# Two places of count keys in a graph-network kernel: one counter for both, or one each

## The chip, the cores and the metric

The kernel runs on one core of a Trainium2 chip. What counts is the time of one execution on the device, in microseconds (us). Before the change the median of three runs is 1840.04 us (1839.89 to 1840.95).

## The reference, cut to what matters

There are 6250 nodes with 256 features and 106,250 edges, sorted by destination. `h` is the ReLU of the layer-normalized `x`. Two layers follow, and their result is added to `x`:

```python
def layer(z, l):
    logits = z @ envW[l] + envb[l]                     # 256 -> 4 experts
    weights = softmax(logits)
    agg = segment_sum(z[src], dst) / max(count(dst), 1)
    combined = concatenate([agg, z])                   # 512
    outputs = einsum('nd,kdo->nko', combined, W[l]) + z[:, None, :]
    return relu(einsum('nk,nko->no', weights, outputs))
```

The expensive parts are the mean over a node's edges (`agg`) and the product of the 512 combined features with four experts' weights.

## The kernel before, in words

Nodes are cut into 49 blocks of 128. For each block TensorE (PE) sums the neighbours' rows in one of two ways.

- **Sparse blocks** (33): the source rows of the block's edges come in units of 2 x 128 edges, fetched by indirect DMAs that GpSimd (POOL) issues into a ring of 12 units (L713, two DMAs a unit). VectorE (DVE) makes one-hot matrices of the destinations (`compare`, L865), and PE multiplies one-hot by rows (L1295, L1300, four matmuls a unit). The one-hots stand in ten places; the pair of places 7 and 8, with place 9, is filled by `compare_next(..., 2)`.
- **Dense blocks** (16): a matrix of edge counts (128 nodes of the block by all nodes) is multiplied by all node features, which lie in SBUF (`group_sum`, L1333, L1335). ScalarE (ACT) turns the counts from bytes into floats in two stage buffers (`fill_stage`, L1075).

The counts themselves are made once, in layer 0, by products of two bf16 one-hot matrices: `win_lo` (position within the block) and `win_key` (window and source). DVE makes them in `window_keys` (L916, L919). PE multiplies them window by window, two windows to a pair (`window_pair`, L1346), and ACT moves each pair from PSUM to SBUF as bytes (`move_pair`, L1087, L1090, L1092). A dense block has 13 pairs, in group 0 (7 pairs) and group 1 (6 pairs). The SBUF tiles `win_lo` and `win_key` hold one group: a **small place** (pairs 0 and 1, four windows) and a **large place** (pairs 2 and up: ten windows in group 0, eight in group 1). `window_keys(dn, g, i)` fills place `i` for group `g` of dense block `dn`; PE waits for the small place before pair 0 and for the large one before pair 2 (`s_key[0]`, `s_key[1]`). That a place may be overwritten is told by one semaphore, `s_keyfree`: ACT adds 2 when PE has summed the last pair of a group, and each fill takes 1.

Each layer has a prologue and then 16 rounds of a loop of three slots. A slot of PE's queue holds a block's eight weight products (`product(0)` to `product(7)`, L1366, two matmuls each) with the sums of the next block between them:

- `first_slot` (k = 0 on the other engines): products 2 to 7, nine or more units of the ring, and in layer 0 the six pairs of group 1: `pair(0)` stands between `product(4)` and unit 7, `pair(1)` after unit 8, `pair(2)` after `product(5)` and a tenth unit if there is one, then the transposition of the next block's features (`turn_z`, L1269), which waits for DVE's `z_in`.
- `dense_slot` (k = 1): a dense block's 49 products with counts and eight units.
- `rest_slot` (k = 2): in layer 0 the seven pairs of group 0, among the eight products, for the next round's dense block.

The order on every engine is written out by hand and static; engines wait only on semaphores. Around the change DVE's order in slot k = 0 is: read two numbers of dense blocks from SBUF (`dense_no`, L671), `take_logits` (L941, L943), `compare_next` (L865), `take_weights` (the softmax weights, L947, L948), small place of group 1, wait for ACT's scaled `z` and `keep_z` (L927, makes `z_in`), large place of group 1, `combine_half(0)` (L953). Both places of group 0 are filled in slot k = 1. In slot k = 2 there is no fill; `split` (L974, L976) stands ahead of `keep_z`. ACT's order in slot k = 2 is `move_pair(0, 0)`, `exps`, `move_pair(0, 1)`, and so on.

These are the lines of the fill that wait and signal:

```python
a, b = (0, 2) if i == 0 else (2, PAIRS_IN[g])
take(dve, s_keyfree)
```

Of the kernel before, what the change touches and what calls it, by code (L numbers as in the profile page):

```python
# [23 lines left out]
PER_ROUND = 2  # L24
# [14 lines left out]
def gnn_kernel(nc, x, src, dst, W, envW, envb, out):  # L39
# [63 lines left out]
    with ctx:  # L103
# [88 lines left out]
        s_ohr = sem("more_onehots_ready")  # L192
        s_ohf = sem("other_onehots_free")
        s_key = [sem(f"keys{i}_ready") for i in range(2)]
        s_keyfree = sem("keys_free")
        s_win = [sem(f"window_pair{p}_summed") for p in range(2)]
        s_wfree = [sem(f"window_pair{p}_free") for p in range(2)]
        s_evac = sem("window_pair_moved")
# [442 lines left out]
        with main_ctx:  # L641
# [57 lines left out]
            with nc.Block() as block:  # L699
# [71 lines left out]
                def _(dve):  # L771
# [81 lines left out]
                    dve.sem_inc(s_mixfree[0], 1)  # L853
                    dve.sem_inc(s_mixfree[1], 1)
                    dve.sem_inc(s_lgfree, 1)
                    dve.sem_inc(s_keyfree, 2)

                    others_from = dve.alloc_register("others_from")
                    others_to = dve.alloc_register("others_to")
# [49 lines left out]
                    def window_keys(dn, g, i):  # L909

                        a, b = (0, 2) if i == 0 else (2, PAIRS_IN[g])
                        take(dve, s_keyfree)
                        w = nc.s_assert_within(dve.snap(dn * WPB + 2 * (PAIR_FROM[g] + a)), 0, WINS - 2 * (b - a),
                                               skip_runtime_bounds_check_because="windows of one block")
                        n = 2 * (b - a)
                        nc.vector.tensor_tensor(  # L916
                            win_lo[:, 2 * a:2 * b, :], lo16[:].unsqueeze(1).to_broadcast([P, n, P]),
                            lo_w[:, bass.ds(w, n)].unsqueeze(2).to_broadcast([P, n, P]), ALU.is_equal)
                        nc.vector.tensor_tensor(  # L919
                            win_key[:, 2 * a:2 * b, :], key16[:].unsqueeze(1).to_broadcast([P, n, KEYS]),  # L920
                            key_w[:, bass.ds(w, n)].unsqueeze(2).to_broadcast([P, n, KEYS]),
                            ALU.is_equal).then_inc(s_key[i], 1)
# [56 lines left out]
                    for l in range(L):  # L979
# [13 lines left out]
                        take_mean(l, sparse_block(dve, zero, 0), 0)  # L993
                        compare_first(sparse_block(dve, zero, 1), wide=True)
                        compare_more()
                        with dve.Fori(0, rounds) as r:
                            dn = dense_no(dve, r)
                            dn1 = dense_no(dve, r + 1)
                            for k in range(ORDER):
                                following = sparse_block(dve, r, k + 1)  # L1000
                                take_logits(l)
                                if k == 0:
                                    compare_next(following, 2)
                                elif k == DENSE_AT:
                                    compare_next(following, 0)
                                take_weights()
                                if k == DENSE_AT:
                                    compare_next(following, 1)
                                    compare_next(following, 2)
                                if first and k == 0:  # L1010
                                    window_keys(dn, 1, 0)
                                elif k == 0:
                                    compare_rest()
                                if k == DENSE_AT + 1:
                                    compare_rest()
                                if first and k:
                                    split()
                                if not first and k <= DENSE_AT:
                                    for g in range(0 if k == 0 else FIRST_GROUPS, FIRST_GROUPS if k == 0 else XG):
                                        dve.wait_ge(s_zload[g], 16)  # L1020
                                take(dve, s_zs)
                                keep_z(block_of(dve, r, dn, k + 1))
                                if first and k == 0:
                                    window_keys(dn, 1, 1)
                                    compare_rest()
                                if first and k == DENSE_AT:
                                    window_keys(dn1, 0, 0)
                                    window_keys(dn1, 0, 1)
                                combine_half(0)
                                take_mean(l, block_of(dve, r, dn, k + 1), bank_of(k))  # L1030
                                if first and k == DENSE_AT:
                                    dve.sem_inc(s_zused, 1)
                                if k < PER_ROUND and k != DENSE_AT:
                                    compare_first(sparse_block(dve, r, k + 2 if k < DENSE_AT else k + 1))
                                elif k == PER_ROUND:
                                    more = dve.snap(r + 1)
                                    with dve.If(more < rounds):
                                        compare_first(sparse_block(dve, more, 1), wide=True)
                                combine_half(1)
                                if k == PER_ROUND:  # L1040
                                    with dve.If(more < rounds):
                                        compare_more()
                                if not first:
                                    result()
                            if first:
                                split()
# [12 lines left out]
                def _(act):  # L1059
# [18 lines left out]
                    def move_pair(g, j):  # L1078

                        p = j % 2  # L1080
                        take(act, s_win[p])
                        if j == PAIRS_IN[g] - 1:
                            act.sem_inc(s_keyfree, 2)
                        at = 2 * WIN * (PAIR_FROM[g] + j)
                        two = win_ps[p][:, 0:2 * KEYS].rearrange("p (v c n) -> p c v n", v=2, n=WIN)
                        if at + 2 * WIN <= P:
                            nc.scalar.activation(counts_sb[:, :, at:at + 2 * WIN].rearrange(  # L1087
                                "p c (v n) -> p c v n", n=WIN), two, ACT.Copy).then_inc(s_evac, 1)
                        else:
                            nc.scalar.activation(counts_sb[:, :, at:at + WIN], two[:, :, 0, :],  # L1090
                                                 ACT.Copy).then_inc(s_evac, 1)
                            nc.scalar.activation(counts_sb[:, :, at + WIN:P], two[:, :, 1, 0:P - at - WIN],  # L1092
                                                 ACT.Copy).then_inc(s_evac, 1)
                            take(act, s_evac)
                        take(act, s_evac)
                        act.sem_inc(s_wfree[p], 1)
# [461 lines left out]
```

## Time and profile before

| | |
|---|---|
| median of three runs | 1840.04 us |
| profiled execution, from its first to its last instruction (span) | 1839.2 us |
| runs' median beside that span | 0.84 us more, 0.05% |
| PE busy / POOL busy / DVE busy / ACT busy | 87% / 66% / 49% / 31% of the span |
| mean granted clock of PE | 0.969 of full speed |
| layer 0, from the first round's dense sums on | about 54.6 us a round |
| layer 1 | about 47.9 us a round |

Shares of busy time are averages over the whole execution. PE is the busiest engine. Its clock has two levels here, 2.4 GHz (1.00 in the profile) and 1.2 GHz (0.50). A bracket at the end of a row gives how long the engine stood idle before it and what ended that: "PEq L101" or "DVEq L101" is a wait on a semaphore in the engine's own queue. An engine that is idle costs nothing unless the others wait for it.

### The profile page before, as it was taken

What the parts mean: (1) busy time and instruction counts of PE and PEld (TensorE: products, weight loads), DVE (VectorE), ACT (ScalarE), POOL (GpSimd) and SP (SyncE); (2) the same over time, 40 slices, a digit from 0 to 9 for tenths busy, and PEclk for the clock granted to TensorE, in tenths of its full rate; (3) what the DMA queues carried; (4) which work ended last, traced back from release to release, by engine and by line L of the source; (5) the groups of instructions that cost most, each with busy time, mean ns of one, the idle gap of its engine ahead of it and who ended that gap; (6) DMA issues with size and microseconds to landing.
All of it is one profiled execution on the core that took longest, in us unless ns stands there. A gap on an engine that the chain in (4) does not pass through costs nothing. (4 is left out here: it accounts for less than half of the span.)

```text
span 1839.2 us, 36146 instructions
## 1 busy us (share of the span) xinstructions
PE 1598.5 (87%) x8502; PEld 1124.8 (61%) x8503; DVE 895.0 (49%) x2024; ACT 572.7 (31%) x1254; POOL 1214.2 (66%) x1187
## 2 busy tenths in 40 slices
PE   1059999999999999999998389999999999999998
PEld 1036665666666666666665266666666666667665
DVE  6665565655565565555564224334443333443333
ACT  4414333334434333433333022222222222222222
POOL 1377776766776676676663677666666666666764
PEclk9989999999999999999999599999999999999999
DMA  7877766666666666666656987677777777777775
GB/s 218 284 216 227 215 206 186 189 180 195 206 191 197 193 175 194 205 195 197 193 173 215 382 259 244 214 221 220 220 221 222 220 220 220 219 216 215 225 219 150
DMA packets 160202, 393.34 MB, mean 214 GB/s; under 512 B 36989, under 2 KB 61080, under 8 KB 160180
## 3 DMA queue, kind: packets, MB, share of 16 engines
q0 software_dynamic: 92544, 302.70, 55.2%
q10 hardware_dynamic: 35112, 61.46, 9.4%
q1 hardware_dynamic: 32524, 28.91, 5.1%
q8 instruction: 11, 0.18, 0.0%
q14 instruction: 11, 0.09, 0.0%
HBM read 347.61 MB, written 45.37 MB: 214 GB/s over the span
## 5 line engine op out<-in xcount | busy, mean ns | idle before, releaser
L713 POOL DMA_INDIRECT ring<-zp_dram,gather_idx x1152 | 1196.1, 1038 | 535.8 <-issue 271.6
L1333 PE MATMUL agg_ps<-zp,stage 128*128 128x258 f32 x1568 | 447.3, 322 | 23.6 <-PEq L101 23.6
L1366 PE MATMUL mix_ps<-w_sb,turned_m 128*128 128x512 f32 x784 | 405.4, 617 | 16.0 <-PEq L101 14.8
L1295 PE MATMUL agg_ps<-ring,onehot 128*128 x1248 | 398.5, 346 | 23.8 <-PEq L101 17.0
L1366 PE MATMUL mix_ps<-w_sb,turned_z 128*128 128x512 f32 x784 | 400.9, 611 | 10.8 <-PEq L101 10.8
L1335 PE MATMUL agg_ps<-zp,stage 128*128 128x256 f32 x1568 | 384.6, 281 | 0.0
L1075 ACT ACTIVATE stage<-counts_sb 128x512 fp32r<-128x512 uint8 (+1 forms) x416 | 247.1, 605 | 387.5 <-ACTq L101 386.6
L1333 PEld LDWEIGHTS agg_ps<-zp,stage 128*128 128x128 f32 x1568 | 296.1, 189 | 87.7 <-issue 83.9
L1300 PE MATMUL agg_ps<-ring,onehot 128*128 x1248 | 328.2, 289 | 0.0
L1335 PEld LDWEIGHTS agg_ps<-zp,stage 128*128 128x128 f32 x1568 | 296.4, 189 | 34.5 <-issue 34.5
L1295 PEld LDWEIGHTS agg_ps<-ring,onehot 128*128 128x128 f32 x1248 | 242.7, 194 | 79.2 <-issue 73.1
L865 DVE TENSOR_TENSOR onehot<-nodes,dst_t 128x512 fp32r<-128x512 f32 (+1 forms) x396 | 224.1, 601 | 114.5 <-issue 89.4
L1300 PEld LDWEIGHTS agg_ps<-ring,onehot 128*128 128x128 f32 x1248 | 243.5, 195 | 30.4 <-issue 30.4
L953 DVE SCALAR_TENSOR_TENSOR mix<-mix_ps,wts,mix 128x256 f32<-128x256 f32 x392 | 188.9, 482 | 123.5 <-DVEq L101 97.1
L1366 PEld LDWEIGHTS mix_ps<-w_sb,turned_m 128*128 128x128 f32 x784 | 130.2, 196 | 66.9 <-issue 64.2
L1087 ACT ACTIVATE counts_sb<-win_ps 128x490 uint8<-128x490 f32 x199 | 118.9, 597 | 140.3 <-ACTq L101 139.7
L1366 PEld LDWEIGHTS mix_ps<-w_sb,turned_z 128*128 128x128 f32 x784 | 127.2, 193 | 52.6 <-issue 52.2
L947 DVE RECIPROCAL rsum<-ex 128x1 f32<-128x1 f32 x98 | 15.9, 163 | 256.4 <-DVEq L101 256.2
L1116 ACT ACTIVATE turned_m<-turn_ps 128x256 f32<-128x256 f32 x98 | 37.1, 378 | 325.3 <-ACTq L101 325.3
L1346 PEld LDWEIGHTS win_ps<-win_key,win_lo 128*128 128x128 bf16 x430 | 39.7, 103 | 160.4 <-issue 156.4
L1346 PE MATMUL win_ps<-win_key,win_lo 128*128 128x245 bf16 x430 | 85.2, 288 | 47.9 <-PEq L101 47.9
L936 DVE TENSOR_SCALAR mean<-agg_ps,rcnt 128x256 f32<-128x256 f32 x98 | 47.4, 484 | 156.7 <-DVEq L101 156.6
(157 smaller groups left out, 944.4 us busy)
## 6 DMA issues: line engine op xcount, KB each, us to landing
ring<-zp_dram,gather_idx POOLq DMA_INDIRECT x1152, 3.8
zp_dram<-zp SPq DMA_DIRECT2D x7, 1792.0 KB, 7.3
a_dram<-counts_sb ACTq DMA_DIRECT2D x16, 784.0 KB, 4.9
zp_dram<-parts ACTq DMA_DIRECT2D x49, 256.0 KB
zp<-zp_dram SPq DMA_DIRECT2D x4, 1792.0 KB, 16.3
counts_sb<-a_dram ACTq DMA_DIRECT2D x17, 400.0 KB, 6.4
parts<-in_x ACTq DMA_DIRECT2D x48, 128.0 KB
counts_sb<-a_dram ACTq DMA_DIRECT2D x16, 384.0 KB, 5.4
```

The lines of the kernel that those rows point to most:

```text
L713: pool.indirect_dma_start(out=ring[:, k, t, 0:2 * D].bitcast(F32), out_offset=None, in_=zp_dram[l], in_offset=bass.IndirectOffsetOnAxis(ap ...
L865: return nc.vector.tensor_tensor(onehot[:, place:place + units, :, :].rearrange("p u t n -> p (u t) n"), nodes[:].unsqueeze(1).to_broadcas ...
L936: nc.vector.tensor_scalar(mean[:], agg_ps[:, bank, 0:D], rcnt[:, bass.ds(blk, 1)], None, ALU.mult).then_inc(s_mean, 1)
L953: ins = nc.vector.scalar_tensor_tensor(out=mix[:], in0=mix_ps[i][:, k * D:(k + 1) * D], scalar=wts[:, i * (K // 2) + k:i * (K // 2) + k + ...
L1075: nc.scalar.activation(stage[:, g % 2, 0:n, :], counts_sb[:, g * STAGE:g * STAGE + n, :], ACT.Copy).then_inc(s_staged, 1)
L1087: nc.scalar.activation(counts_sb[:, :, at:at + 2 * WIN].rearrange("p c (v n) -> p c v n", n=WIN), two, ACT.Copy).then_inc(s_evac, 1)
L1295: mm = pe.matmul(agg_ps[:, bank, 0:D + 2], onehot[:, place, t, :], rows[:, :, D:2 * D + 2], start=place == 0 and t == 0, stop=True, skip_g ...
L1300: mm = pe.matmul(agg_ps[:, bank, 0:D], onehot[:, place, t, :], rows[:, :, 0:D], start=False, stop=True, skip_group_check=True)
L1333: pe.matmul(agg_ps[:, bank, 0:D + 2], stage[:, g % 2, i, :], zp[:, c, D:2 * D + 2], start=c == 0, stop=True, skip_group_check=True)
L1335: mm = pe.matmul(agg_ps[:, bank, 0:D], stage[:, g % 2, i, :], zp[:, c, 0:D], start=False, stop=True, skip_group_check=True)
L1346: mm = pe.matmul(win_ps[p][:, v * KEYS:(v + 1) * KEYS], win_lo[:, 2 * j + v, :], win_key[:, 2 * j + v, :], start=True, stop=True, skip_gro ...
L1366: mm = pe.matmul(mix_ps[i][:, :], (turned_z, turned_m)[what][:, c, :], w[:, i * HALF:(i + 1) * HALF], start=what == 0 and c == 0, stop=wha ...
```

## The change

`s_keyfree` becomes two semaphores, one for each place. ACT releases the small place when pair 1 is summed, and the large one with the last pair of the group. The small place of group 1 is filled in slot k = 2 of the round before (for the first round: ahead of the loop), behind `split` and ahead of `keep_z`. The large place of group 1 is filled right behind the softmax weights, ahead of `keep_z`. The reading of the two block numbers moves behind `take_logits`, in both layers. PE's and ACT's orders stay as they are.

```diff
-        s_keyfree = sem("keys_free")
+        s_keyfree = [sem(f"keys{i}_free") for i in range(2)]
...
-                    dve.sem_inc(s_keyfree, 2)
+                    for i in range(2):
+                        dve.sem_inc(s_keyfree[i], 1)
...
-                        take(dve, s_keyfree)
+                        take(dve, s_keyfree[i])
...
                         compare_more()
+                        if first:
+                            window_keys(zero, 1, 0)
                         with dve.Fori(0, rounds) as r:
-                            dn = dense_no(dve, r)
-                            dn1 = dense_no(dve, r + 1)
                             for k in range(ORDER):
+                                take_logits(l)
+                                if k == 0:
+                                    dn = dense_no(dve, r)
+                                    dn1 = dense_no(dve, r + 1)
                                 following = sparse_block(dve, r, k + 1)
-                                take_logits(l)
...
                                 if first and k == 0:
-                                    window_keys(dn, 1, 0)
+                                    window_keys(dn, 1, 1)
...
                                 if first and k:
                                     split()
+                                if first and k == PER_ROUND:
+                                    window_keys(dn1, 1, 0)
...
                                 keep_z(block_of(dve, r, dn, k + 1))
                                 if first and k == 0:
-                                    window_keys(dn, 1, 1)
                                     compare_rest()
...
                         take(act, s_win[p])
+                        if j == 1:
+                            act.sem_inc(s_keyfree[0], 1)
                         if j == PAIRS_IN[g] - 1:
-                            act.sem_inc(s_keyfree, 2)
+                            act.sem_inc(s_keyfree[1], 1)
```

The order of instructions says more than the diff. The names are those of tiles; `ISA` and `REGISTER_ALU` are register work, `TENSOR_LOAD plan` reads a number from SBUF into a register. Line numbers after the change are a few higher.

DVE, slot k = 0 of layer 0, from the softmax weights on. Before:

```order
L948 TENSOR_SCALAR wts<-ex,rsum 128x5
L916 ISA
L916 TENSOR_TENSOR win_lo<-lo,lo_w 128x512
L919 REGISTER_ALU
L919 TENSOR_TENSOR win_key<-key,key_w 128x980
L927 ISA
L927 TENSOR_TENSOR z_in<-zp 128x256
L916 ISA
L916 TENSOR_TENSOR win_lo<-lo,lo_w 128x1024
L919 REGISTER_ALU
L919 TENSOR_TENSOR win_key<-key,key_w 128x1960
```

With the change:

```order
L949 TENSOR_SCALAR wts<-ex,rsum 128x5
L917 ISA
L917 TENSOR_TENSOR win_lo<-lo,lo_w 128x1024
L920 REGISTER_ALU
L920 TENSOR_TENSOR win_key<-key,key_w 128x1960
L928 ISA
L928 TENSOR_TENSOR z_in<-zp 128x256
```

The small fill (512 and 980 elements) is gone from this slot, and the large one (1024 and 1960) now stands ahead of `z_in`.

DVE, slot k = 2 of layer 0, from `split` on. Before:

```order
L974 TENSOR_SCALAR parts<-z_out 128x256
L976 TENSOR_TENSOR parts<-z_out,parts 128x256
L927 ISA
L927 TENSOR_TENSOR z_in<-zp 128x256
L953 SCALAR_TENSOR_TENSOR mix<-mix_ps,wts,mix 128x256 x2
```

With the change:

```order
L975 TENSOR_SCALAR parts<-z_out 128x256
L977 TENSOR_TENSOR parts<-z_out,parts 128x256
L917 ISA
L917 TENSOR_TENSOR win_lo<-lo,lo_w 128x512
L920 REGISTER_ALU
L920 TENSOR_TENSOR win_key<-key,key_w 128x980
L928 ISA
L928 TENSOR_TENSOR z_in<-zp 128x256
```

The small fill stands here now, for the next round, ahead of `z_in`.

DVE, start of slot k = 0. Before:

```order
L671 TENSOR_LOAD plan
L671 ISA x3
L671 TENSOR_LOAD plan
L671 ISA x2
L941 TENSOR_TENSOR logits<-lg_ps,bias 128x4
L943 TENSOR_REDUCE negmax<-logits 128x1
L674 ISA
L674 TENSOR_LOAD plan
L674 ISA x2
```

With the change:

```order
L942 TENSOR_TENSOR logits<-lg_ps,bias 128x4
L944 TENSOR_REDUCE negmax<-logits 128x1
L671 ISA
L671 TENSOR_LOAD plan
L671 ISA x3
L671 TENSOR_LOAD plan
L671 ISA x2
L674 ISA
L674 TENSOR_LOAD plan
L674 ISA x2
```

Three reads from SBUF now stand between the logits and the comparisons, where one stood.

## Rows read from the trace of the kernel before

**Rows 1.** The page's first line.

```profile
span 1839.2 us, 36146 instructions
```

**Rows 2.** PE's waits, 130 to 1000 us: total us, times, longest.

```profile
PE win_ps L1346 <- PEq L101: 44.1, 15, 3.0
```

**Rows 3.** PE in time order, first slot of one round: start us, us, instruction, [idle before].

```profile
404.88 1.02 PE L1366 MATMUL mix_ps<-w_sb,turned_m 128*128 128x512 f32 x2
408.78 0.37 PE L1346 MATMUL win_ps<-win_key,win_lo 128*128 128x245 bf16 x2 [2.88 <-PEq L101]
409.29 0.38 PE L1295 MATMUL agg_ps<-ring,onehot 128*128 x1
...
410.03 0.55 PE L1295 MATMUL agg_ps<-ring,onehot 128*128 x1
...
413.80 0.39 PE L1346 MATMUL win_ps<-win_key,win_lo 128*128 128x245 bf16 x2
414.03 0.38 PE L1269 MATMUL turn_ps<-ident,z_in 128*128 128x128 f32 x2
```

**Rows 4.** DVE in time order, the same slot.

```profile
401.91 0.43 DVE L976 TENSOR_TENSOR parts<-z_out,parts 128x256 f32<-128x256 f32 x1
403.93 0.16 DVE L941 TENSOR_TENSOR logits<-lg_ps,bias 128x4 f32<-128x4 f32 x1 [1.59 <-DVEq L101]
...
405.34 1.03 DVE L865 TENSOR_TENSOR onehot<-nodes,dst_t 128x256 fp32r<-128x256 f32 x2 [0.85 <-issue]
...
406.85 0.69 DVE L916 TENSOR_TENSOR win_lo<-lo,lo_w 128x512 bf16<-128x512 f16 x1
407.46 1.17 DVE L919 TENSOR_TENSOR win_key<-key,key_w 128x980 bf16<-128x980 f16 x1
408.55 0.42 DVE L927 TENSOR_TENSOR z_in<-zp 128x256 f32 x1
408.89 1.22 DVE L916 TENSOR_TENSOR win_lo<-lo,lo_w 128x1024 bf16<-128x1024 f16 x1
410.02 2.19 DVE L919 TENSOR_TENSOR win_key<-key,key_w 128x1960 bf16<-128x1960 f16 x1
```

**Rows 5.** Stretches: busy us (count) of PE, PEld, DVE, ACT, POOL; PEclk; DMA; GB/s.

```profile
187.00:1000.00 813.00, 754.15 (x4046) 524.97 (x4045) 467.72 (x952) 312.20 (x674) 555.37 (x503) 0.97 0.64 192
1083.00:1830.00 747.00, 714.47 (x3840) 511.22 (x3840) 290.90 (x730) 185.99 (x437) 515.39 (x527) 1.00 0.72 219
...
410.10:413.50 3.40, 3.40 (x10) 2.22 (x11) 2.12 (x2) 0.58 (x1) 2.79 (x3) 0.50 0.52 154
...
116.60:126.70 10.10, 6.26 (x23) 3.53 (x23) 7.38 (x17) 4.18 (x10) 8.05 (x7) 0.50 0.60 168
```

**Rows 6.** DVE in time order, first slot of a round with nine units.

```profile
516.06 0.69 DVE L916 TENSOR_TENSOR win_lo<-lo,lo_w 128x512 bf16<-128x512 f16 x1
```

**Rows 7.** PE in time order, the same slot.

```profile
522.79 0.38 PE L1269 MATMUL turn_ps<-ident,z_in 128*128 128x128 f32 x2
```

**Rows 8.** DVE, last slot (k = 2) of a round of layer 0.

```profile
446.04 0.43 DVE L976 TENSOR_TENSOR parts<-z_out,parts 128x256 f32<-128x256 f32 x1
```

**Rows 9.** PE, the same slot.

```profile
448.94 0.38 PE L1269 MATMUL turn_ps<-ident,z_in 128*128 128x128 f32 x2
```

**Rows 10.** ACT, the same slot: `move_pair(0, 1)`.

```profile
444.57 0.64 ACT L1087 ACTIVATE counts_sb<-win_ps 128x490 uint8<-128x490 f32 x1
```

**Rows 11.** PE's waits, 1083 to 1830 us (layer 1).

```profile
PE mix_ps L1366 <- PEq L101: 14.8, 15, 1.0
```

**Rows 12.** POOL's groups, 420 to 474 us (one round): busy us, mean ns, idle before.

```profile
L713 POOL DMA_INDIRECT ring<-zp_dram,gather_idx x34 | 36.9, 1086 | 17.7 <-POOLq L101 9.4 <-issue 8.2
```

**Rows 13.** POOL in time order, beside the fills of rows 4.

```profile
404.72 0.94 POOL L713 DMA_INDIRECT ring<-zp_dram,gather_idx  x1 [0.30 <-PE agg_ps L1300]
...
407.49 1.96 POOL L713 DMA_INDIRECT ring<-zp_dram,gather_idx  x1 [0.30 <-issue]
```

**Rows 14.** PE, prologue of layer 0.

```profile
117.92 0.98 PE L1346 MATMUL win_ps<-win_key,win_lo 128*128 128x245 bf16 x4 [2.72 <-PEq L101]
```

## The prediction

> **What bounds the kernel now.** The chain of waits holds only its last piece, so I went by PE, the busiest engine, and asked where it stands idle in the span of 1839.2 us [rows 1]. The list of its waits in layer 0 has one large entry: the product of count keys waits 15 times, 44.1 us in all [rows 2], once in each round but the first. PE's time order shows the place. `product(4)` ends at 405.90, and `pair(0)` starts at 408.78, after 2.88 us idle [rows 3]. DVE's time order shows for whom: its small fill runs from 406.85 to 407.46 + 1.17 = 408.63, and PE goes on 0.15 us later [rows 4]. That fill stands behind the comparison (to 405.34 + 1.03 = 406.37) and the softmax weights. So in this slot DVE's chain from logits to small fill ends last, and PE, with all its other work of the round, waits for it.
>
> The table of stretches shows a second cost. From 410.10 to 413.50, right behind the wait, PE's granted clock is 0.50 (1.2 GHz). Over rounds 1 to 15 (187 to 1000 us) its mean is 0.97, and in layer 1 it is 1.00 [rows 5]. One stretch of 3.4 us a round gives 15 x 3.4 x 0.5 / 813 = 0.031, the whole of what is missing from 1.00. Half speed for 3.4 us loses 1.7 us of work a round. In the order of time each such stretch follows the wait for keys, and there is none elsewhere in these rounds.
>
> **The change part by part.** I take the round of rows 3 and 4 and follow it to `turn_z`, from where every engine's order is as before.
>
> *Reading the block numbers later.* Before, DVE's logits start 1.59 us after `split` (401.91 + 0.43), and the comparison 0.85 us after `negmax` [rows 4]. The change puts the same reads behind the logits; all of them lie between `split` and the comparison in both orders. The comparison moves by nothing, or by 0.1 us for one more register instruction. Bounds: earlier by 0.2, later by 0.5 (half the 0.85 us that one read with its register work takes here). I take +0.1: it ends at 406.47. In layer 1 the same move is worth nothing: PE's wait there is for the transposed mean, ahead of `product(4)` (15 times, at most 1.0 us) [rows 11], and the comparison is wanted only behind it. Cover gone: at worst 0.5 x 15 = 7.5 us.
>
> *`pair(0)` no longer waits.* It starts at 405.9. The next thing missing is the one-hots of unit 7: the comparison's end, 406.47, plus the 0.5 us from `pair(0)`'s release to unit 7's first matmul (408.78 to 409.29 [rows 3]), so 406.97. PE waits there about 0.9 us. Unit 7 takes 0.74 (409.29 to 410.03), unit 8 some 0.5 at full clock, `pair(1)` 0.2, `product(5)` 0.9 (1.02 less its overlap), the tenth unit 0.5. PE asks for `pair(2)` at 409.8.
>
> *The large fill moves ahead.* It takes 408.89 to 410.02 + 2.19 = 412.21, 3.32 us [rows 4]. Behind the weights it starts where the small one started, 406.85 + 0.1, and ends at 410.27. `pair(2)` starts at 410.42: a second wait of 0.6 us. The large place is free long before, since its release comes with the last pair of the slot before.
>
> *`keep_z` moves behind it.* `z_in` takes 0.42 us and overlaps the fill by 0.1, so it ends at 410.6; with 0.12 us for the signal (keys took 0.15) `turn_z` starts at 410.72. Before it started at 414.03 [rows 3]. **Gain: 3.31 us** in a round with ten units in this slot; there are 6 of these among the 15.
>
> In a round with nine units the small fill starts at 516.06 [rows 6] and `turn_z` at 522.79 [rows 7]. Now: 516.06 + 0.1 + 3.32 + 0.33 + 0.12 = 519.93. **Gain: 2.86 us**, in 9 rounds. Here PE has no tenth unit and waits 1.1 us for the large fill.
>
> As a check the other way: 2.88 + 1.7 us vanish, waits of 0.9 and 0.6 us come new, which makes 3.1.
>
> *The small fill in slot k = 2* costs DVE nothing in sum. It starts behind `split`, at 446.04 + 0.43 = 446.47 [rows 8], and takes 1.8, so `z_in` ends at 448.6 at the latest, and PE's `turn_z` starts at 448.94 [rows 9]. That cover is only 0.3 us. The release is early enough: ACT's `move_pair(0, 1)`, ahead of which it now stands, starts at 444.57 [rows 10]. Bounds: 0 and, if the signal and DVE's queue cost 0.3 more than I count, 0.3 us a round. I take 0.1, 1.5 us in all. Late next would be `turn_z`, then `copy_z`, then the next logits.
>
> *Round 0* waits for gathers, and its pairs of group 1 do not wait for keys (15 waits, not 16) [rows 2]; the small fill ahead of the loop delays DVE's first logits by 1.8 us under that. Nothing.
>
> Behind `turn_z` the order and all distances stay, so the gain is kept. **Sum:** 6 x 3.31 + 9 x 2.86 - 1.5 = 44.1 us. This presumes that the clock stays at 2.4 GHz. What speaks for it: layer 1 has waits of 1.0 us before `product(4)` and similar ones later in each round [rows 11], and its clock is 1.00 throughout [rows 5]. The new waits are of that size. The span becomes 1839.2 - 44.1 = 1795.1; the runs' median stood 0.84 above the span, so I forecast **1796 us**.
>
> The Trainium skill (TensorE: Matmul & The Clock Gate, section "Why this matters for your kernels") names a longer idle gap than the 2.88 us seen here as the one to avoid. By that the half-clock stretch would not be the wait's doing and would outlive it, which is the first rival. The trace speaks against it: the stretch follows this wait each time.
>
> **The rivals.**
>
> *The half clock stays.* The new waits, 0.9 and then 0.6 to 1.1 us within 5 us, still bring down the clock for 3.4 us. If that falls ahead of the second wait, it is half hidden (0.6 to 1.1 us are lost); if behind it, 1.7. That is 15 x 0.6 = 9 to 15 x 1.7 = 26 us given back: 1805 to 1822 us. Against it stands layer 1, though its two waits lie farther apart. Chance 0.08.
>
> *More than forecast.* If the large fill or the comparison came sooner than I count, the whole of wait and half clock could go, 15 x (2.93 + 1.7) = 69 us: 1771 us. Against it stands DVE's chain of 3.32 us, whose length comes from rows; only the part above 1789 is likely. Chance 0.03 for anything below 1789.
>
> *The gathers become the pace.* A round is now to take 54.6 - 2.9 = 51.7 us. POOL's 34 gathers take 36.9 us with 0.30 of issue each, 47.1 us [rows 12]. A gather beside a fill takes 1.96 us against 0.94 [rows 13]. From a mean of 1.22 us (51.7 / 34 - 0.30) POOL sets the pace, and at 1.30 nothing is gained: 1840 us. The mean is 1.086 now, the same fills run in each round, and layer 1 with as many gathers runs at 47.9 us a round. Chance 0.02. The Trainium skill (SBUF — State Buffer, section "SBUF: two separate sides") says that VectorE and GpSimd share one pair of ports, which one holds for a whole instruction. The 1.96 us agree, and by it the slow gathers only move with the fills.
>
> *Slower: a long half clock.* In the prologue a wait of 2.72 us [rows 14] with shorter ones behind it went with a clock of 0.50 for 10.1 us [rows 5]. If two waits in close succession did that in every round, 5.1 us of work would be lost, some 0.9 of it hidden in the second wait. That is 4.2 against a gain of 2.9: 15 x 1.3 = 19 us slower, 1859 us. It decides from a half-clock stretch of about 7.7 us (2 x (2.9 + 0.9)). Against it: PE is idle for much less here than there. Chance 0.02.
>
> *That the change doesn't do what it says* can be left out: in the order of instructions both fills stand where it says, and both releases come before they are asked for.
>
> **How the numbers follow.** The forecast case holds 0.85: the sum with its bounds, 1796 less 7 (0.5 us a round, if clock and signals are kinder) to 1796 plus 12 (7.5 for the comparison, 3 for slot k = 2, 1 for the rest). I close the range at 1789 and 1809, which takes in the mild end of the first rival. A measurement of this kernel can tell 0.2% from no change, 3.7 us. Faster is the forecast with the first two rivals, 0.96; the same 0.02; slower 0.02.
>
> **What would show it.** In the changed kernel's profile: PE's waits on `win_ps` fall from 44.1 to some 15 x 0.9 = 13 us, now before `pair(2)`; a new wait of about 0.9 us stands before unit 7 (L1295's group); mean clock of the rounds of layer 0 near 1.00; a round of 51.5 us on average; no new wait before `turn_z` in slot k = 2; layer 1 unchanged at 47.9 us a round. I am wrong if a half-clock stretch is left in each round, if `turn_z` of slot k = 2 starts more than 0.3 us later against its neighbours, or if POOL's idle time goes to nothing.

## The result, and the profile after

The changed kernel takes 1798.78 us in the median of four runs (1796.7 to 1802.87), the kernel before 1839.97 us in the same number. The ratio is 0.9778, 95% interval 0.9766 to 0.979: 41 us or 2.2% faster. The forecast was 1796 us.

The page of the changed kernel, its first lines:

```profile
span 1795.8 us, 36215 instructions
## 1 busy us (share of the span) xinstructions
PE 1577.5 (88%) x8502; PEld 1112.0 (62%) x8503; DVE 888.8 (49%) x2026; ACT 572.7 (32%) x1254; POOL 1202.2 (67%) x1187
```

The span is 43.4 us shorter than before [rows 1]. Where it went is read from the first dense sum (L1333 before, L1340 after) of rounds 0 and 15 and of layer 1. Three rows of PE's time order before:

```profile
146.59 0.36 PE L1333 MATMUL agg_ps<-zp,stage 128*128 128x258 f32 x1 [0.70 <-PEq L101]
...
965.91 0.36 PE L1333 MATMUL agg_ps<-zp,stage 128*128 128x258 f32 x1 [0.64 <-PEq L101]
...
1074.90 0.69 PE L1333 MATMUL agg_ps<-zp,stage 128*128 128x258 f32 x1
```

and the same three after:

```profile
144.08 0.36 PE L1340 MATMUL agg_ps<-zp,stage 128*128 128x258 f32 x1 [0.70 <-PEq L101]
...
919.10 0.36 PE L1340 MATMUL agg_ps<-zp,stage 128*128 128x258 f32 x1 [0.65 <-PEq L101]
...
1031.39 0.36 PE L1340 MATMUL agg_ps<-zp,stage 128*128 128x258 f32 x1 [3.50 <-PEq L101]
```

| stretch | before, us | after, us | difference |
|---|---|---|---|
| up to round 0's dense sums | 146.6 | 144.1 | -2.5 |
| rounds 1 to 15 of layer 0 | 819.3 | 775.0 | -44.3 |
| from there to layer 1's dense sums | 109.0 | 112.3 | +3.3 |
| the rest (layer 1) | 764.3 | 764.4 | +0.1 |

The forecast's sum was made for the second line and said 44.1. Within these rounds the gain lies in one place. In the mean of the 15 rounds PE takes 40.98 us from the dense sums to the end of `product(4)` before and 40.97 after, and 5.80 and 5.79 us from the first slot's `turn_z` to the next dense sums; between the two, where keys, unit 7 and `turn_z` are waited for, it takes 7.84 us before and 4.90 after.

PE's waits of layer 0 after the change (130 to 958 us), against the 44.1 us of [rows 2]:

```profile
PE agg_ps L1302 <- PEq L101: 16.0, 17, 2.4
PE win_ps L1353 <- PEq L101: 11.3, 15, 1.0
```

The keys cost 11.3 us of waiting now. The first row is the wait for the one-hots of unit 7 (15 times about 0.84 us) and two waits in round 0. PE's time order of one round with ten units, the place of [rows 3]:

```profile
390.67 1.02 PE L1373 MATMUL mix_ps<-w_sb,turned_m 128*128 128x512 f32 x2
391.53 0.38 PE L1353 MATMUL win_ps<-win_key,win_lo 128*128 128x245 bf16 x2
392.74 0.38 PE L1302 MATMUL agg_ps<-ring,onehot 128*128 x1 [0.84 <-PEq L101]
...
396.27 0.37 PE L1353 MATMUL win_ps<-win_key,win_lo 128*128 128x245 bf16 x2 [0.48 <-PEq L101]
396.61 0.41 PE L1276 MATMUL turn_ps<-ident,z_in 128*128 128x128 f32 x2
```

DVE in the same slot, the place of [rows 4]:

```profile
388.73 0.16 DVE L944 TENSOR_REDUCE negmax<-logits 128x1 f32<-128x4 f32 x1 [0.24 <-DVEq L101]
391.21 1.03 DVE L866 TENSOR_TENSOR onehot<-nodes,dst_t 128x256 fp32r<-128x256 f32 x2 [2.32 <-issue]
...
392.72 1.29 DVE L917 TENSOR_TENSOR win_lo<-lo,lo_w 128x1024 bf16<-128x1024 f16 x1
393.94 2.19 DVE L920 TENSOR_TENSOR win_key<-key,key_w 128x1960 bf16<-128x1960 f16 x1
396.05 0.41 DVE L928 TENSOR_TENSOR z_in<-zp 128x256 f32 x1
```

`pair(0)` follows `product(4)` without a wait. The comparison ends at 392.24 and unit 7 starts 0.50 us later; the large fill ends at 396.13 and `pair(2)` starts 0.14 later; `z_in` ends at 396.46 and `turn_z` starts 0.15 later. Each of the three new chains ends last where the forecast put it. New to the eye is the 2.32 us ahead of the comparison: three reads of numbers from SBUF with DVE idle beside them.

The granted clock, in the stretch of rounds 1 to 15 (182 to 960 us; columns as in [rows 5]):

```profile
182.00:960.00 778.00, 739.55 (x4071) 515.50 (x4070) 465.64 (x963) 313.72 (x679) 545.99 (x507) 1.00 0.68 204
```

It was 0.97. No stretch at 1.2 GHz is left in these rounds.

### The profile page after: what moved, and what is told of

Its sections match the earlier page's. It is cut to its first block and busy times, and to the rows that moved or that the text cites. A ratio compares the mean times of both kernels' runs of the same rounds, so it can differ in the third digit from the quotient of the medians.

```text
span 1795.8 us, 36215 instructions
## 1 busy us (share of the span) xinstructions
PE 1577.5 (88%) x8502; PEld 1112.0 (62%) x8503; DVE 888.8 (49%) x2026; ACT 572.7 (32%) x1254; POOL 1202.2 (67%) x1187
## 5 line engine op out<-in xcount | busy, mean ns | idle before, releaser
L713 POOL DMA_INDIRECT ring<-zp_dram,gather_idx x1152 | 1184.0, 1028 | 504.8 <-issue 275.0
L1340 PE MATMUL agg_ps<-zp,stage 128*128 128x258 f32 x1568 | 448.1, 323 | 26.5 <-PEq L101 26.5
L1302 PE MATMUL agg_ps<-ring,onehot 128*128 x1248 | 390.6, 341 | 27.0 <-PEq L101 21.8
L1373 PE MATMUL mix_ps<-w_sb,turned_m 128*128 128x512 f32 x784 | 393.1, 601 | 16.0 <-PEq L101 14.8
L1340 PEld LDWEIGHTS agg_ps<-zp,stage 128*128 128x128 f32 x1568 | 296.6, 189 | 91.2 <-issue 87.4
L1307 PE MATMUL agg_ps<-ring,onehot 128*128 x1248 | 322.8, 285 | 0.0
L1302 PEld LDWEIGHTS agg_ps<-ring,onehot 128*128 128x128 f32 x1248 | 238.9, 191 | 80.9 <-issue 75.0
L1307 PEld LDWEIGHTS agg_ps<-ring,onehot 128*128 128x128 f32 x1248 | 239.0, 191 | 29.1 <-issue 29.1
L920 DVE TENSOR_TENSOR win_key<-key,key_w 128x980 bf16<-128x980 f16 x67 | 120.7, 1801 | 0.0
```

The costliest lines, as they stand in the source:

```text
L713: pool.indirect_dma_start(out=ring[:, k, t, 0:2 * D].bitcast(F32), out_offset=None, in_=zp_dram[l], in_offset=bass.IndirectOffsetOnAxis(ap ...
L920: nc.vector.tensor_tensor(win_key[:, 2 * a:2 * b, :], key16[:].unsqueeze(1).to_broadcast([P, n, KEYS]), key_w[:, bass.ds(w, n)].unsqueeze( ...
L1302: mm = pe.matmul(agg_ps[:, bank, 0:D + 2], onehot[:, place, t, :], rows[:, :, D:2 * D + 2], start=place == 0 and t == 0, stop=True, skip_g ...
L1307: mm = pe.matmul(agg_ps[:, bank, 0:D], onehot[:, place, t, :], rows[:, :, 0:D], start=False, stop=True, skip_group_check=True)
L1340: pe.matmul(agg_ps[:, bank, 0:D + 2], stage[:, g % 2, i, :], zp[:, c, D:2 * D + 2], start=c == 0, stop=True, skip_group_check=True)
L1373: mm = pe.matmul(mix_ps[i][:, :], (turned_z, turned_m)[what][:, c, :], w[:, i * HALF:(i + 1) * HALF], start=what == 0 and c == 0, stop=wha ...
```

## The experiments

"Rounds 1 to 15" is the time from round 0's first dense sum to round 15's, read from each profile as above. "Stretches" counts those with a clock of 0.50 within it.

| kernel | median, us | ratio to before (95%) | rounds 1 to 15, us | stretches |
|---|---|---|---|---|
| before | 1840 | 1 | 819.3 | 15 |
| changed | 1798.8 | 0.978 (0.977 to 0.979) | 775.0 | 0 |
| e1 numbers first | 1801.4 | 0.978 (0.976 to 0.980) | 774.8 | 0 |
| e2 large fill behind z_in | 1820.6 | 0.989 (0.987 to 0.990) | 800.3 | 6 |
| e3 clock kept (on before) | 1821.0 | 0.989 (0.988 to 0.991) | 802.3 | 0 |
| e5 numbers late | 1783.1 | 0.969 (0.967 to 0.971) | 758.3 | 0 |
| e6 one comparison more | 1815.7 | 0.987 (0.985 to 0.989) | 792.9 | 6 |
| e7 two comparisons more | 1829.7 | 0.994 (0.993 to 0.996) | 809.3 | 11 |
| e9 large fill in two | 1786.8 | 0.971 (0.969 to 0.972) | 761.6 | 0 |
| e8 numbers late and in two | 1768.9 | 0.961 (0.960 to 0.963) | 742.6 | 0 |
| e12 counted at once (on changed) | 1795.3 | 0.975 (0.974 to 0.977) | 775.1 | 0 |
| e11 all three | 1762.5 | 0.958 (0.956 to 0.959) | 742.5 | 0 |
| e10 reload late (on before) | 1840.5 | 1.000 (0.999 to 1.001) | 817.4 | 14 |

### e1: does the place of the reads ahead of the comparison matter?

```diff
+                                if k == 0:
+                                    dn = dense_no(dve, r)
+                                    dn1 = dense_no(dve, r + 1)
                                 take_logits(l)
-                                if k == 0:
-                                    dn = dense_no(dve, r)
-                                    dn1 = dense_no(dve, r + 1)
```

> The changed kernel with one part undone: the two block numbers are read ahead of the logits again. My theory: the reads lie between split and the comparison in either order, so the one-hots of places 7 to 9 come at the same time (0.1 us earlier at most) and the time is the changed kernel's, some 1798 us, within 2 us. Rival: the later reads are part of the gain, since logits and exp come 1.5 us sooner; then up to 15 x 1.5 = 22 us are lost, 1820 us.

Rounds 1 to 15 take 774.8 us against 775.0. The third part of the change is worth nothing there; the gain is the fills'. The median is 1801.4 us, more than the 2 us off that I had allowed, but the runs of the two kernels overlap (1797.3 to 1801.6 us and 1796.7 to 1802.9), so no difference is shown.

### e2: is the large fill's new place part of the gain?

```diff
-                                if first and k == 0:
-                                    window_keys(dn, 1, 1)
-                                elif k == 0:
+                                if not first and k == 0:
                                     compare_rest()
...
                                 if first and k == 0:
+                                    window_keys(dn, 1, 1)
                                     compare_rest()
```

> The changed kernel with the large fill behind z_in again, so that only the small fill is moved forward. My theory: nearly the whole gain is the small fill's. z_in takes 0.34 us of DVE ahead of the fill, so pair(2) starts 0.34 us later, but turn_z then follows it by 0.2 us and no longer waits for z_in: 0.2 us a round, 3 us, 1801 us. Rival: the large fill's new place carries a real part of the gain; then 1 us or more a round is lost, 1813 us or more.

My theory missed by 20 us and the rival holds. DVE in a round of this kernel shows the first half of the reason:

```profile
398.47 0.23 DVE L949 TENSOR_SCALAR wts<-ex,rsum 128x5 f32<-128x5 f32 x1 [0.16 <-DVEq L101]
399.61 0.42 DVE L928 TENSOR_TENSOR z_in<-zp 128x256 f32 x1 [0.91 <-DVEq L101]
399.95 1.22 DVE L917 TENSOR_TENSOR win_lo<-lo,lo_w 128x1024 bf16<-128x1024 f16 x1
```

`keep_z` waits for ACT to scale the old `z_in` with the weights, which takes it until 399.33 (ACT's row, next), so the fill starts 1.25 us behind the weights and not 0.34:

```profile
398.82 0.51 ACT L1140 ACTIVATE mix<-z_in,wts 128x256 f32<-128x256 f32 x1 [3.43 <-ACTq L101]
```

I had counted `z_in`'s own time and forgotten the wait in front of it. That makes a round 52.5 us instead of 51.5. The second half is the clock. From round 7 on, in six rounds with nine units, PE waits 0.8 us before unit 7 and 2.1 us before `pair(2)`, and the clock falls behind the latter:

```profile
508.70 0.37 PE L1352 MATMUL win_ps<-win_key,win_lo 128*128 128x245 bf16 x2 [2.12 <-PEq L101]
...
509.19 1.91 PE L1372 MATMUL mix_ps<-w_sb,turned_m 128*128 128x512 f32 x2
```

The two matmuls of a product take 1.91 us there, 1.03 at full clock. Those rounds last 54.5 us: 2.7 longer than in the changed kernel (51.8), the other nine 1.0 longer, 6 x 2.7 + 9 x 1.0 = 25 us, which is what the table shows. Rounds 1, 3 and 6, with the same two waits, kept the clock, and so did the six rounds with ten units, whose second wait is 1.6 us.

### e3: what was the clock's share before?

```diff
                             product(4)
+                            if build:
+                                for _ in range(12):
+                                    pe.matmul(agg_ps[:, 0, 2 * P + P:], ident[:], ident[:], start=False, stop=True,
+                                              skip_group_check=True)
                             pair(0)
```

> The kernel before, with 12 matmuls of identity by identity (added into columns of a PSUM bank that nobody reads) put between product(4) and pair(0) of layer 0's first slot. They take some 2.6 us, less than the wait of 2.9 us, so the wait for keys is as long as before but PE is not idle in it. My theory: the half-clock stretch comes from the idle time, so it goes, and 15 x 1.7 = 25 us with it: 1815 us, with a granted clock of 1.00 in the rounds. Rival: the stretch has another cause or the wait alone makes the cost; then the time stays at 1840 us and the clock at 0.97.

PE's time order in the place of the wait:

```profile
345.68 1.02 PE L1366 MATMUL mix_ps<-w_sb,turned_m 128*128 128x512 f32 x2
346.53 2.84 PE L1397 MATMUL agg_ps<-ident 128*128 128x128 f32 x24
349.63 0.37 PE L1346 MATMUL win_ps<-win_key,win_lo 128*128 128x245 bf16 x2 [0.26 <-PEq L101]
...
353.21 0.37 PE L1346 MATMUL win_ps<-win_key,win_lo 128*128 128x245 bf16 x2
```

All 15 stretches at 1.2 GHz are gone, though `pair(0)` waits for its keys as long as before: the idle time is what brings the clock down. The direction of my theory holds, the size does not. The rounds give 17.0 us (819.3 to 802.3), 1.1 each and not 1.7. `pair(2)` now comes 3.58 us behind `pair(0)`, just as long as the large fill takes behind the small one: in rounds with nine units PE waits up to 0.5 us for it, which eats part of what the clock gives back. These nine rounds gain 0.9 us each, the six with ten units, without that wait, 1.4.

So of the change's 44.3 us, 17 are to be had by keeping the clock alone; the other 27 need the keys sooner.

### e5: the reads between the logits and the comparison

```diff
                                 take_logits(l)
-                                if k == 0:
-                                    dn = dense_no(dve, r)
-                                    dn1 = dense_no(dve, r + 1)
                                 following = sparse_block(dve, r, k + 1)
                                 if k == 0:
                                     compare_next(following, 2)
+                                    dn = dense_no(dve, r)
...
+                                if k == 0:
+                                    dn1 = dense_no(dve, r + 1)
```

> The changed kernel with the block numbers read still later: that of this round behind the comparison of places 7 to 9, that of the next round behind the large fill. The reads then run in DVE's queue while it computes. My theory: what is left of the waits (0.85 us before unit 7, 0.5 to 1.0 us before pair(2)) is DVE's chain with 1.4 us of reads in it; one-hots, weights, large fill and z_in come about 1.3 us sooner, the wait before unit 7 goes, and the gain is up to 1.3 us a round, 20 us: 1779 us. Rival: ACT's moves of the pairs or its stages end last as soon as pair(2) comes sooner; then half or less of it is gained, 1788 to 1798 us.

1783 us: 16 us less than the changed kernel, where I had named up to 20, and clear of the rival's 1788 to 1798. The wait before unit 7 is gone; the one before `pair(2)` is now the largest:

```profile
PE win_ps L1353 <- PEq L101: 14.1, 15, 1.2
```

### e6 and e7: where does the clock fall?

```diff
                         else:
+                            for _ in range(more):        # 1 in e6, 2 in e7; layer 0, k = 0 only
+                                settle(compare(lo + 7, 7, 2))
                             compare(lo + 9, 9)
```

> The changed kernel with the comparison of places 7 and 8 made once more in layer 0's first slot, ahead of the real one: DVE's chain there is 0.8 us longer, so PE waits 1.65 us before unit 7 instead of 0.85. My theory: every later step of the round shifts by 0.8 us, 15 x 0.8 = 12 us, 1811 us, and the clock holds, since the waits (1.65, then 0.5 to 0.95) are still shorter together than the 2.9 us in which it fell and the 0.8 + 2.1 us in which it fell in some rounds of the run with the large fill behind z_in. Rival: the comparison is not on the path of the round (the large fill alone is), then the time stays at 1799 us.

> The same with two additional comparisons: PE waits 2.45 us before unit 7 and then 0.5 to 0.95 us. My theory: 15 x 1.6 = 24 us for the longer chain, 1823 us, and in most rounds the half-clock stretch comes back, now partly hidden in the second wait (0.8 to 1.7 us lost in each), 12 to 25 us more: 1835 to 1848 us, with a mean clock near 0.97 in these rounds. Rival: only a wait of 2.9 us in one piece brings the clock down; then 1823 us and a clock of 1.00.

PE's wait before unit 7, one row of each kernel's list of waits (e6, then e7):

```profile
PE agg_ps L1304 <- PEq L101: 27.5, 15, 1.9
```

```profile
PE agg_ps L1304 <- PEq L101: 37.8, 17, 2.7
```

In e7 one more wait of 2.7 us before unit 7 stands in another row of the list. The comparison is on the path, as the first theory said. Rounds without a fall are about 1.0 us longer in e6 and 1.8 in e7. But both numbers missed on the clock. In e6 it fell in 6 of 15 rounds, which I had said it would not, and it did so behind the first wait alone, ahead of the place of the second. One such round, PE's rows and a stretch (columns as in [rows 5]):

```profile
452.09 0.38 PE L1304 MATMUL agg_ps<-ring,onehot 128*128 x1 [1.85 <-PEq L101]
...
453.42 0.63 PE L1355 MATMUL win_ps<-win_key,win_lo 128*128 128x245 bf16 x2
```

```profile
453.40:456.80 3.40, 3.40 (x11) 1.77 (x10) 3.09 (x4) 1.67 (x3) 2.79 (x3) 0.50 0.66 222
```

The other nine rounds kept the clock behind the same wait. e6 is 1815.7 us and not 1811: some 3 us of the miss are the clock's, the rest comes from the comparison, which cost 1.0 us a round and not 0.8. In e7 it fell in 11 rounds, yet cost less than I charged, 1829.7 us and not 1835 or more: at half speed PE comes later to `pair(2)`, whose keys are then there, and the second wait shrinks from 11.3 us to 3.1 us in all.

### e9 and e8: the large fill in two pieces

```diff
-                        a, b = (0, 2) if i == 0 else (2, PAIRS_IN[g])
-                        take(dve, s_keyfree[i])
+                        a, b = ((0, 2), (2, 4 if g else PAIRS_IN[0]), (4, PAIRS_IN[1]))[i]
+                        if i < 2:
+                            take(dve, s_keyfree[i])
...
                                 keep_z(block_of(dve, r, dn, k + 1))
                                 if first and k == 0:
+                                    window_keys(dn, 1, 2)
                                     compare_rest()
...
-                        if j == 0 or j == 2:
+                        if j == 0 or j == 2 or (g and j == 4):
                             take(pe, s_key[j // 2])
```

e9 is the changed kernel with this alone, e8 is e5 with it.

> The changed kernel with nothing but the large fill of group 1 in two pieces, as in the run before. The wait before unit 7 (0.85 us) stays, the one before pair(2) (0.47 us in 6 rounds, 0.95 us in 9) goes: 11 us less than the changed kernel, 1787 us. Rival: z_in or the second piece comes too late for turn_z or pair(4); then 1795 us or more.

> The kernel with the late reads of the block numbers (1783 us), and in it the large fill of group 1 in two pieces with a semaphore each: pairs 2 and 3 behind the softmax weights, pairs 4 and 5 behind z_in. My theory: pair(2) waits only for four windows (1.8 us of DVE instead of 3.3), so its wait of 0.66 to 1.10 us goes: 6 x 0.66 + 9 x 1.10 = 14 us, 1769 us. Rival: ACT's chain of moving pairs, copying and staging ends last then, or the gathers do (the last ones already land 2 to 4 us later in the round in each faster kernel); then 1776 to 1783 us.

Both numbers came as forecast: 1786.8 us for 1787 and 1768.9 us for 1769. PE's waits in e8's rounds 1 to 15:

```profile
PE agg_ps L1342 <- PEq L101: 7.9, 15, 0.7
PE win_ps L1355 <- PEq L101: 1.4, 8, 0.2
```

The keys no longer cost anything to speak of. What is left is the wait for ACT's first stage of counts ahead of the dense sums, which the kernel before had too.

### e10, e11, e12: the 3.3 us given back between the layers

SyncE reloads layer 1's features (L696) behind the last gathers. Its rows before, and after the change:

```profile
989.18 0.33 SPq L736 DMA_DIRECT2D gather_idx<-src_dram  x1
990.21 0.99 SPq L752 DMA_DIRECT2D gather_idx<-src_dram  x2
998.06 10.31 SPq L696 DMA_DIRECT2D zp<-zp_dram  x4
```

```profile
945.00 0.33 SPq L736 DMA_DIRECT2D gather_idx<-src_dram  x1
946.03 1.00 SPq L752 DMA_DIRECT2D gather_idx<-src_dram  x2
953.89 9.38 SPq L696 DMA_DIRECT2D zp<-zp_dram  x4
```

Counted from round 15's first dense sum, the reload starts at 32.2 us before and at 34.8 after: the last gathers have not gained as much as PE has (the last one of the layer starts at 19.5 us before and at 22.0 after). Between lines L752 and L696 SyncE takes two semaphores 16 times in a loop, some 6 us. Three kernels tested what the start is worth. e10 delays it in the kernel before; e11 (on e8) and e12 (on the changed kernel) replace the loop:

```diff
-                            with sp.Fori(0, rounds_of(sp)) as _:
-                                take(sp, s_zkept)
-                                take(sp, s_zused)
+                            more = rounds_of(sp)
+                            take(sp, s_zkept, R)
+                            take(sp, s_zused, R)
+                            with sp.If(more > R):
+                                with sp.Fori(R, more) as _:
+                                    take(sp, s_zkept)
+                                    take(sp, s_zused)
```

and e10 has

```diff
                                 take(sp, s_idx[0][h], 16)
+                                if h == 0:
+                                    sp.dma_start(gather_idx[:, 0:half], src_dram[:, 0:half]).then_inc(s_late, 16)
+                                    sp.wait_ge(s_late, 16)
```

> The kernel before, with one small list of indices loaded twice by SyncE at the end of layer 0, ahead of the reload of layer 1's features, so that the reload starts 2 to 4 us later. My theory: from the start of the reload to layer 1's first dense sums it is 76 to 77 us in every profile so far, since the DMA engines are full in between, so the whole delay shows in the time: 1842 to 1844 us, and the first dense sums of layer 1 stand 111 to 113 us behind the last ones of layer 0 instead of 109. Rival: the reload is not on the path (the weights of layer 1, asked for 20 us later, are), then the time stays at 1840 us.

> The kernel with late reads and the large fill in two pieces (1769 us), and in it SyncE takes the 16 rounds' counts of both semaphores at once instead of in a loop of 16 turns, which takes 6.1 us behind the last gathers. My theory: the reload starts some 5.8 us sooner and the whole of it is gained, 1763 us. Rival: the weights of layer 1 or the stores of the last blocks set the pace then, and 0 to 3 us are gained, 1766 to 1769 us.

> The changed kernel with the same edit and no other: 5.8 us less than the changed kernel, 1793 us, by my theory; 1796 to 1799 us by the rival.

SyncE in e11:

```profile
918.26 1.35 SPq L752 DMA_DIRECT2D gather_idx<-src_dram  x2
920.63 10.01 SPq L696 DMA_DIRECT2D zp<-zp_dram  x4
```

| kernel | reload starts | layer 1's dense sums start | between |
|---|---|---|---|
| before | +32.2 | +109.0 | 76.8 |
| e10 | +34.1 | +109.5 | 75.4 |
| changed | +34.8 | +112.3 | 77.5 |
| e12 | +29.1 | +109.2 | 80.1 |
| e8 | +37.8 | +113.4 | 75.6 |
| e11 | +31.8 | +107.4 | 75.6 |

e11 gains all of it: 1762.5 us, 6.5 less than e8, and the best of these kernels. e12 gains 3.4 of 5.8 us, in the time only at the edge of the noise (1794.8 to 1798.0 us against 1796.7 to 1802.9), in the profile 3.1 us in this stretch. e10's delay of 1.9 us moves the dense sums by 0.5 us and does not show in its time (its interval reaches from -1 to +2.4 us). So an earlier reload is worth something, but my theory of a fixed distance is not held up: it varies by 5 us.

The traces say why. ACT asks for layer 1's weights, for the rest of the reload and then for layer 1's counts, and from the reload's start to the dense sums the DMA engines are busy all the time (mean share 0.99 before, 998 to 1075 us). ACT's first stage of layer 1's counts, before and after:

```profile
1072.56 0.38 ACT L1112 ACTIVATE turned_z<-turn_ps 128x256 f32<-128x256 f32 x1 [15.10 <-ACTq L101]
1072.85 1.14 ACT L1075 ACTIVATE stage<-counts_sb 128x512 fp32r<-128x512 uint8 x2
```

```profile
1024.25 0.38 ACT L1119 ACTIVATE turned_z<-turn_ps 128x256 f32<-128x256 f32 x1 [9.98 <-ACTq L101]
1030.62 0.63 ACT L1080 ACTIVATE stage<-counts_sb 128x512 fp32r<-128x512 uint8 x1 [5.98 <-ACTq L101]
```

Before, the stage follows `turned_z` at once; after, ACT waits 5.98 us for it and PE 3.50 us (the last of its rows above), which is the 3.3 us. In e5, e9 and e10 the landing is in the trace: the second load of counts lands 0.2 us ahead of this stage. Before, it lands at +104.1 (counted as in the table), 2.8 us ahead of its stage; that room takes up most of e10's delay. In e12 the wait is gone. In e8 layer 1's first product waits 28.7 us, in e11 9.5 us, each time until 0.1 to 0.2 us behind the landing of the last weights. No run moves these loads by themselves, so this is read from traces and not tested.

## Why the prediction was right

**"In this slot DVE's chain ends last."** Right; e1, e5, e6 and e9 lengthen and shorten that chain, and the rounds follow each time.

**The sum for the rounds.** 44.1 us forecast, 44.3 measured. The terms: wait before unit 7 0.9, measured 0.84; second wait 0.6 and 1.1, measured 0.48 and 0.95; large fill 3.32, measured 3.41 with one overlap; comparison 0.1 us later, and the reads' order worth nothing (e1). PE's waits for keys fell to 11.3 us, forecast 13. A round is 51.7 us, as the sum has it (the list of signs said 51.5).

That the sum came out within 0.2 us is partly luck. Rounds with ten units gained 3.25 us each where 3.31 was forecast, those with nine 2.76 where 2.86 was. That is 1.3 us less in all, and the 1.5 us charged for slot k = 2, which did not fall due, made up for it.

**The clock stays at full speed.** Right, 1.00 in rounds 1 to 15. It had less reserve than layer 1's rows made it look: one more microsecond of waiting (e2, e6) and it fell in 6 rounds. The first rival, given 0.08, was near. The charge of 1.7 us a round for the clock before was an upper bound; e3 shows 1.4 in rounds where nothing is waited for behind it and 0.9 where the large fill hides part of it, 1.1 in the mean. It stood only in the check, not in the sum. (The last rival's 2 x (2.9 + 0.9) is 7.6 us and not 7.7; nothing hangs on it.)

**The large fill's place.** The text counted its move as a term without saying how much of the gain hangs on it. My own expectation for e2 put that at 3 us; it is 22. The step that failed there is `keep_z`'s wait for ACT.

**The small fill in slot k = 2.** Hidden, as said. DVE's and PE's rows there, the places of [rows 8] and [rows 9]:

```profile
429.62 1.17 DVE L920 TENSOR_TENSOR win_key<-key,key_w 128x980 bf16<-128x980 f16 x1
430.70 0.42 DVE L928 TENSOR_TENSOR z_in<-zp 128x256 f32 x1
```

```profile
431.54 0.38 PE L1276 MATMUL turn_ps<-ident,z_in 128*128 128x128 f32 x2
```

`turn_z` starts 0.42 us behind `z_in`, where it needs 0.15, so no term of 1.5 us was due; the stretch from the dense sums to `product(4)`, in which this slot lies, is as long as before.

**"Round 0: nothing."** It shows 2.5 us less. The other kernels' profiles have round 0's dense sums between 144 and 148 us, with and without the early fill, so I take this for scatter.

**"Behind `turn_z` all distances stay, so the gain is kept."** Wrong between the layers, by 3.3 us. POOL's queue and the work that hangs on its last gather were not followed to the end of the layer: the reload starts 2.6 us later against PE, and ACT and PE then wait for layer 1's counts, as read above.

**The step from span to median.** I added 0.84 us. Every run of which both are known lies 1.8 to 2.3 us above its span, the changed kernel's profiled one too (1797.94 against 1795.8), so the profiled execution before was probably itself 1.0 to 1.5 us above the median. That is up to half of the 2.8 us by which the forecast fell short of the median; the rest lies within the runs' own range.

**The gathers.** No pace-setter: 34 or 35 gathers a round with a mean of 1077 ns against 1086, and still idle time:

```profile
L713 POOL DMA_INDIRECT ring<-zp_dram,gather_idx x35 | 37.7, 1077 | 15.1 <-issue 8.8 <-POOLq L101 6.3
```

## What to carry to other kernels

Where the busiest engine waits once a round for another, write down that engine's queue from the last thing both share to the release, and move out of it what is not needed yet: other work of the same engine, and reads of numbers into registers, which stall it (2.32 us for three of them here; moving two was worth 1.1 us a round). Split a buffer's release and its fill by what is used first; a fill of 3.3 us whose first half alone was awaited cost 0.5 to 1 us a round. Moving an instruction ahead of another also moves it ahead of that one's wait; look for the wait first, since it may be longer than the instruction.

## What the runs showed of the hardware that I had not expected

TensorE's clock fell to 1.2 GHz for 3.4 us behind single waits of 2.9 to 3.0 us in all 15 rounds before, in 11 rounds of e7 with a first wait of about 2.65 us (once for 6.8 us), in 6 rounds of e6 behind a wait of 1.85 us, in 6 of e2 behind one of 2.1 us that followed one of 0.8, and in none of the changed kernel, whose waits are 0.84 and up to 0.97 us. Rounds with the same waits differed in it, within one kernel too: 9 of e6's 15 rounds kept the clock. e10 leaves these rounds as they were before, yet its first one kept full speed behind the longest of the waits:

```profile
192.36 0.37 PE L1350 MATMUL win_ps<-win_key,win_lo 128*128 128x245 bf16 x2 [3.05 <-PEq L101]
```

What decides between such rounds was not tested. The Trainium skill (TensorE: Matmul & The Clock Gate, section "Why this matters for your kernels") advises against idle gaps a little longer than 2.9 us; in the traces here shorter ones already cost clock in some rounds. e3 shows that matmuls without use in their place, 24 in 2.84 us, keep it.

The half-clock stretch cost less than half its length in e3's comparison: 1.4 us of 3.4 in rounds where nothing is waited for behind it, 0.9 where another engine's chain ends just behind it.
